# Selected LSTM after a graph network: gates i, f, g and the output gate as two sets of products, and one check of the guess behind both

## The reference

```python
def step(carry, x_t):
    h, c = carry
    logits = concatenate([h, c, x_t]) @ W_sel.T + b_sel
    s = argmax(logits)
    i, f, g, o = split(x_t @ W_ih[s].T + h @ W_hh[s].T + b_ih[s] + b_hh[s], 4)
    c2 = sigmoid(f) * c + sigmoid(i) * tanh(g)
    h2 = sigmoid(o) * tanh(c2)
    return (h2, c2), h2
```

## Time and profile before

| | us |
|---|---|
| median of three runs | 7,709.52 |
| the profiled execution | 7,713.46 |
| its span, first to last instruction | 7,711.7 |
| 256 steps with a unit (window 1,488 to 2,839) | 1,351 |
| 994 steps without (window 2,843 to 7,690) | 4,847 |

### The profile page before, as it was taken

One profiled execution on the slowest core, in us unless ns is written; L12 is line 12 of the kernel. 1 busy time (PEld: TensorE's weight loads), 2 busy tenths in 40 slices (PEclk: granted clock), 3 DMA queues, 4 the chain that ended last, 5 costly groups with the idle time before them and its releaser, 6 DMA issues. The chain is left out here.

```text
span 7711.7 us, 250693 instructions
## 1 busy us (share of the span) xinstructions
PE 6634.8 (86%) x85214; PEld 3513.4 (46%) x85215; DVE 3545.5 (46%) x16895; ACT 1004.7 (13%) x4031; POOL 945.3 (12%) x2829
## 2 busy tenths in 40 slices
PE   3467998899999998888888888888888888888888
PEld 3433444655555554444444444444444444444444
DVE  5523112355555554444444444444444444444444
ACT  0011001311111111111111111111111111111111
POOL 5703112200000000000000000000000000000000
PEclk6588998999999999999999999999999999999999
DMA  3220001622222210000000000000000000000000
GB/s 83 0 68 0 0 0 40 224 78 81 80 84 77 83 56 8 4 8 4 8 8 4 8 4 8 6 7 8 4 8 7 6 8 4 8 4 8 8 4 24
DMA packets 292938, 220.00 MB, mean 29 GB/s; under 512 B 137196, under 2 KB 268652, under 8 KB 290609
## 3 DMA queue, kind: packets, MB, share of 16 engines
q1 hardware_dynamic: 162612, 160.58, 6.2%
q10 hardware_dynamic: 106110, 59.01, 3.0%
q0 software_dynamic: 24192, 0.10, 1.0%
HBM read 160.28 MB, written 59.36 MB: 28 GB/s over the span
## 5 line engine op out<-in xcount | busy, mean ns | idle before, releaser
L1021 PE MATMUL ps<-WH,hparts 128*17 128x512 f16 x49760 | 2969.1, 380 | 148.9 <-DVE hparts L864 63.7
L1021 PEld LDWEIGHTS ps<-WH,hparts 128*17 128x17 f16 x49760 | 1305.0, 91 | 1316.2 <-DVE hparts L864 242.7
L840 DVE STREAM_TRANSPOSE gateT<-ps 128x512 f32<-128x512 f32 x1250 | 896.0, 717 | 2097.2 <-PE ps L1057 2088.0
L1091 PE MATMUL ps<-WH 128*128 128x512 f16 x4970 | 1246.1, 381 | 0.0
L467 POOL COPY xT<-hfull 128x4 f32 x1250 | 239.9, 192 | 5386.9 <-DVE hparts L862 5386.9
L1008 PE MATMUL ps<-wselT,acts 128*1 128x4 f32 x10000 | 430.5, 166 | 407.1 <-DVE acts L852 407.1
L972 PE MATMUL ps<-O,Adj 128*128 128x512 f16 x3000 | 650.3, 380 | 77.2 <-DVEq L749 77.2
L1091 PEld LDWEIGHTS ps<-WH 128*128 128x128 f16 x4970 | 404.6, 97 | 630.8 <-issue 278.7
L581 ACT ACTIVATE gateT<-gblk 128x16 f32 x1250 | 289.3, 231 | 2660.9 <-DVE pick L835 2618.4
L585 ACT ACTIVATE acts<-gates 128x16 f32<-128x16 f32 x1250 | 269.8, 216 | 2239.8 <-DVE gates L844 2239.8
L1065 PE MATMUL ps<-xT,wih_next 128*128 x2048 | 501.1, 388 | 65.1 <-DMA wih_next<-in_w_ih 34.0
(11 more groups left out here) (141 smaller groups left out, 4547.4 us busy)
## 6 DMA issues: line engine op xcount, KB each, us to landing
wih_next<-in_w_ih SPq DMA_DIRECT2D x256, 256.0 KB, 2.9
gblk<-gate_inputs ACTq DMA_DIRECT2D x48, 800.0 KB, 5.0
gate_inputs<-gx_next SPq DMA_DIRECT2D x64, 500.0 KB, 2.6
wst<-in_w_hh ACTq DMA_DIRECT2D x32, 512.0 KB, 7.6
wih<-in_w_ih SPq DMA_DIRECT2D x16, 1024.0 KB, 8.6
adjacency<-Adj SPq DMA_DIRECT2D x2, 6400.5 KB, 24.7
Adj<-adjacency SPq DMA_DIRECT2D x2, 6400.0 KB, 26.8
gate_inputs<-gstage SPq DMA_DIRECT2D x16, 500.0 KB, 6.0
```

The lines of the kernel that those rows point to most:

```text
L840: dve.transpose(gateT[:, :, 0:32], gate_ps.rearrange("p (c q) -> p c q", q=32)).then_inc(turned, 1)
L1021: nc.tensor.matmul(gate_ps[32 * j:32 * j + 17, :], hparts[:, k, :], WH[:, s * KC + k, part, j, :], start=(k == 0 and part == 0), stop=(k = ...
L1091: nc.tensor.matmul(ps[:, 2, :], WH[:, 0, 0, 0, 0:P], WH[:, 0, 0, 0, :], start=True, stop=True)
```

## The change

- PE's products are split. cell_products computes i, f and g in 384 columns (PIECES reorders WH so that the output gate is last); output_products computes the output gate in 128 columns, into another bank. hparts has two columns instead of 17.
- The branches to the code of the set now stand ahead of the logits, which are repeated in each of the four branches. The guess of the next step is loaded behind the guessed products and ahead of the wait for the pick.
- After the guessed cell products PE waits for the pick and compares. If it differs, cell and output products of the picked set follow (repeated); if not, a semaphore (settled) is raised and branches lead to the output products of the set. There is no seal: the last product of each group raises the semaphore.
- VectorE's cell waits for the guessed products and for settled, then sums rows and columns in one transposing reduction of 384 columns and adds the projected input; then it waits for the output products and does the same with 128 columns. ScalarE has a tanh of its own for the output gate. cprod follows behind both.
- WARM is 3 instead of 5. The splitting of W_hh takes three instructions where it took one. The output gate's rows of the projected input are stored last (a reordering of addresses).

```diff
     EPS = 1e-5
-    WARM = 5
+    WARM = 3
...
+    PIECES = ((0, 2 * P, 0), (2 * P, P, 3 * P), (3 * P, P, 2 * P))
...
-        gateT = sb("gateT", [P, G * SUB, 33], f32)
-        gates = sb("gates", [P, G * SUB], f32)
-        acts = sb("acts", [P, G * SUB + SUB], f32)
+        gx_now = sb("gx_now", [P, G * SUB], f32)
+        hsum = sb("hsum", [P, 3 * SUB], f32)
+        osum = sb("osum", [P, 2, SUB], f32)
+        otan = sb("otan", [P, SUB], f32)
+        gates = sb("gates", [P, 3 * SUB], f32)
+        acts = sb("acts", [P, 4 * SUB], f32)
...
-                    pool.tensor_tensor(WH[:, chunk, 1, j:j + 2, :].rearrange("p a j n -> p (a j n)"),
-                                       wst[:, b, :, :].rearrange("p j n -> p (j n)"),
-                                       WH[:, chunk, 0, j:j + 2, :].rearrange("p a j n -> p (a j n)"),
-                                       ALU.subtract).then_inc(whh_low[b], 1)
+                    for first, size, to in PIECES:
+                        part = pool.tensor_tensor(WH[:, chunk, 1, j:j + 2, to:to + size].rearrange("p a j n -> p (a j) n"),
+                                                  wst[:, b, :, first:first + size],
+                                                  WH[:, chunk, 0, j:j + 2, to:to + size].rearrange("p a j n -> p (a j) n"),
+                                                  ALU.subtract)
+                    part.then_inc(whh_low[b], 1)
...
-                    act.activation(acts[:, 0:G * SUB], gates[:, :], ACT.Tanh, scale=1.0 / GATE_SCALE).then_inc(acts_ready, 1)
-                    act.wait_ge(c_ready, act.snap(i * (2 * TG) + tl + (b * TG + 2)))
-                    act.activation(tanc[:, :], acts[:, G * SUB:G * SUB + SUB], ACT.Tanh, scale=0.5).then_inc(tanc_ready, 1)
+                    act.activation(acts[:, 0:3 * SUB], gates[:, :], ACT.Tanh, scale=1.0 / GATE_SCALE).then_inc(acts_ready, 1)
+                    act.wait_ge(osum_ready, n)
+                    act.activation(otan[:, :], osum[:, 1, :], ACT.Tanh, scale=1.0 / GATE_SCALE).then_inc(otan_ready, 1)
+                    act.wait_ge(c_ready, n)
+                    act.activation(tanc[:, :], acts[:, 3 * SUB:4 * SUB], ACT.Tanh, scale=0.5).then_inc(tanc_ready, 1)
...
-            def cell(t, n, n2):
-                dve.wait_ge(gates_mm, n)
-                dve.transpose(gateT[:, :, 0:32], gate_ps.rearrange("p (c q) -> p c q", q=32)).then_inc(turned, 1)
-                dve.wait_ge(turned, n)
-                dve.wait_ge(gx_set, n)
-                dve.tensor_reduce(gates[:, :], gateT[:, :, 0:33:16], AX.X, ALU.add).then_inc(gates_ready, 1)
-                dve.wait_ge(acts_ready, n)
-                dve.scalar_tensor_tensor(out=cprod[:, :], in0=acts[:, 0:2 * SUB], scalar=1.0, in1=acts[:, 3 * SUB:5 * SUB],
+            def cell(m):
+                dve.wait_ge(guess_mm, m)
+                dve.wait_ge(settled, m)
+                dve.tensor_reduce(hsum[:, :], gate_ps.rearrange("p (c q) -> p c q", q=32), AX.X, ALU.add,
+                                  apply_transpose=True).then_inc(turned, 1)
+                dve.wait_ge(turned, m)
+                dve.wait_ge(gx_set, m)
+                dve.tensor_tensor(gates[:, :], hsum[:, :], gx_now[:, 0:3 * SUB], ALU.add).then_inc(gates_ready, 1)
+                dve.wait_ge(ogate_mm, m)
+                dve.tensor_reduce(osum[:, 0, :], ogate_ps.rearrange("p (c q) -> p c q", q=32), AX.X, ALU.add,
+                                  apply_transpose=True).then_inc(oturned, 1)
+                dve.wait_ge(oturned, m)
+                dve.tensor_tensor(osum[:, 1, :], osum[:, 0, :], gx_now[:, 3 * SUB:4 * SUB], ALU.add).then_inc(osum_ready, 1)
+                dve.wait_ge(acts_ready, m)
+                dve.scalar_tensor_tensor(out=cprod[:, :], in0=acts[:, 0:2 * SUB], scalar=1.0, in1=acts[:, 2 * SUB:4 * SUB],
                                          op0=ALU.add, op1=ALU.mult).then_inc(cprod_ready, 1)
-                dve.tensor_scalar(osig[:, :], acts[:, 2 * SUB:3 * SUB], 1.0, float(2 ** B), ALU.add, ALU.mult).then_inc(osig_ready, 1)
-                dve.wait_ge(cprod_ready, n)
-                dve.scalar_tensor_tensor(out=acts[:, 4 * SUB:5 * SUB], in0=cprod[:, SUB:2 * SUB], scalar=0.5, in1=cprod[:, 0:SUB],
+                dve.wait_ge(cprod_ready, m)
+                dve.scalar_tensor_tensor(out=acts[:, 3 * SUB:4 * SUB], in0=cprod[:, SUB:2 * SUB], scalar=0.5, in1=cprod[:, 0:SUB],
                                          op0=ALU.mult, op1=ALU.add).then_inc(c_ready, 1)
-                dve.wait_ge(osig_ready, n)
-                dve.wait_ge(hist_free, n)
-                dve.tensor_tensor(owsel[:, :, :], osig[:, :].rearrange("p (c a) -> p c a", a=1).broadcast_to([P, SUB, S]),
-                                  wselT[:, SUB:2 * SUB, :], ALU.mult).then_inc(owsel_ready, 1)
-                dve.wait_ge(tanc_ready, dve.snap(t + 2))
+                dve.wait_ge(otan_ready, m)
+                dve.scalar_tensor_tensor(out=owsel[:, :, :], in0=otan[:, :].rearrange("p (c a) -> p c a", a=1).broadcast_to([P, SUB, S]),
+                                         scalar=1.0, in1=wselT[:, SUB:2 * SUB, :], op0=ALU.add, op1=ALU.mult).then_inc(owsel_ready, 1)
+                dve.wait_ge(hist_free, m)
+                dve.tensor_scalar(osig[:, :], otan[:, :], 1.0, float(2 ** B), ALU.add, ALU.mult).then_inc(osig_ready, 1)
+                dve.wait_ge(tanc_ready, m)
+                dve.wait_ge(osig_ready, m)
                 dve.tensor_tensor(hfull[:, :], osig[:, :], tanc[:, :], ALU.mult).then_inc(h_full, 1)
-                dve.tensor_tensor(hparts[:, :, 0], osig[:, :], tanc[:, :], ALU.mult).then_inc(h_full, 1)
-                dve.wait_ge(h_full, n2)
-                dve.tensor_tensor(hparts[:, :, 16], hfull[:, :], hparts[:, :, 0], ALU.subtract).then_inc(h_ready, 1)
-            choose(1, 2)
+                dve.tensor_tensor(hparts[:, :, 0], osig[:, :], tanc[:, :], ALU.mult).then_inc(h_high, 1)
+                dve.wait_ge(h_high, m)
+                dve.tensor_tensor(hparts[:, :, 1], hfull[:, :], hparts[:, :, 0], ALU.subtract).then_inc(h_ready, 1)
+            choose(1)
             dve.sem_inc(unit_out, 1)
             def step(t):
-                n = dve.snap(t + 1)
-                cell(t, n, dve.snap(t * 2 + 2))
-                choose(dve.snap(t + 2), dve.snap(t + 3))
-                return n
+                m = dve.snap(t + 2)
+                cell(m)
+                choose(m)
...
-            def logits(t, n):
+            def logits(n):
                 pe.wait_ge(lx_set, n)
-                pe.wait_ge(lmark_ready, n)
                 nc.tensor.matmul(logit_ps, ones[:, 0:1], lx_now[:, :], start=True, stop=False)
-                pe.wait_ge(c_ready, n)
+                pe.wait_ge(owsel_ready, n)
                 for k in range(SUB):
-                    nc.tensor.matmul(logit_ps, acts[:, G * SUB + k:G * SUB + k + 1], wselT[:, k, :], start=False, stop=False)
-                pe.wait_ge(owsel_ready, n)
+                    nc.tensor.matmul(logit_ps, acts[:, 3 * SUB + k:3 * SUB + k + 1], wselT[:, k, :], start=False, stop=False)
                 pe.wait_ge(tanc_ready, n)
                 for k in range(SUB):
                     last = nc.tensor.matmul(logit_ps, tanc[:, k:k + 1], owsel[:, k, :], start=False, stop=(k == SUB - 1))
                 last.then_inc(logits_mm, 1)
-            def products(s, n, first):
-                if first:
-                    pe.wait_ge(h_ready, n)
+            def cell_products(s, done):
                 for k in range(KC):
                     for part in range(2):
                         for j in range(4):
-                            nc.tensor.matmul(gate_ps[32 * j:32 * j + 17, :], hparts[:, k, :], WH[:, s * KC + k, part, j, :],
-                                             start=(k == 0 and part == 0), stop=(k == KC - 1 and part == 1),
-                                             tile_position=(0, 32 * j))
-            def products_of(chosen, n, first):
-                with pe.If_lt(chosen, 3):
-                    with pe.If_lt(chosen, 2):
-                        products(3, n, first)
+                            last = nc.tensor.matmul(gate_ps[32 * j:32 * j + 2, :], hparts[:, k, :], WH[:, s * KC + k, part, j, 0:3 * P],
+                                                    start=(k == 0 and part == 0), stop=(k == KC - 1 and part == 1),
+                                                    tile_position=(0, 32 * j))
+                last.then_inc(done, 1)
+            def output_products(s):
+                for k in range(KC):
+                    for part in range(2):
+                        for j in range(4):
+                            last = nc.tensor.matmul(ogate_ps[32 * j:32 * j + 2, :], hparts[:, k, :], WH[:, s * KC + k, part, j, 3 * P:4 * P],
+                                                    start=(k == 0 and part == 0), stop=(k == KC - 1 and part == 1),
```

(35 more changed lines are left out.)

85 lines of the change are left out of this document (48 added, 37 removed).

## The result

The changed kernel takes **7,883.4 us**, median of three runs (7,874.0 to 7,890.0), against 7,709.5: a ratio of 1.0224, 95% interval 1.0201 to 1.0247. It is slower by 174 us. The profiled execution has a span of 7,881.6 us against 7,711.7, a difference of 170 us.

A forecast was written before the change was run, and what follows sets the result against it. It took right tail steps as TensorE streaming, then a DVE/ACT chain; unit steps as bound by PE's program order. 7,713.5 - 100 (repeated) + 175 (unit) + 45 (repeated unit) + 10 = 7,843, said as 7,845 us; range 7,620 to 8,150.

The forecast's parts named there:

- The right step of the tail: Steps without a projection unit whose guess was right: claimed unchanged at 4.48 us, the streaming gain going into the check.
- E: Time from P at which PE's sequencer reaches the wait for the pick; forecast 0.86 us in the tail.
- R: Start of VectorE's output reduction, counted from P; forecast P+2.86 us, with the next P at R + 1.58.
- 0.44 us of streaming vanish in the check: 384 columns for 512 in the cell products gain 0.44 us, which in right tail steps goes into the check.
- The unit step: Right step beside a projection unit, issued after the output products: 5.9 against 4.92 us, +0.97 x 180 = +175 us.
- P: Start of a step's cell products; times in a step are counted from it, and a period runs to the next.
- Repeated steps: Steps whose guess was wrong: tail -0.43 us x 232 = -100 us; beside a unit +0.6 x 75 = +45 us.
- Parts at nothing: Terms put at zero: two warm products fewer, splitting W_hh in three, added DVE and ACT semaphores; likewise two weight rows for 17.
- First passage through more code: Extra time when the larger code is first run through, two first compares having taken up to 4.47 us: +10 us.
- Cheaper branches: Rival: the three branches behind the load cost less, sequencer path 0.1 to 0.3 us shorter; say 7,640 us; chance 0.14.
- Products issued one by one: Rival: small output products take 0.10 us a group, R 0.28 us later, +213 us: 8,058; chance 0.12.
- The clock falls: Rival: PE drops to 1.2 GHz under the new load, R moves by 0.9 us, +890: 8,735 us; chance 0.07.

## Why the prediction was right, and where it was off

It said 7,845, faster 0.14, slower 0.78; the time is 7,883, and the mechanism is the one it named.

**The right step of the tail.** Against the means: E 0.839 (0.86 forecast), settled 1.681 (1.69), first reduction 1.791 (1.75), first output product 2.179 (2.15), last one 2.603 (2.57), R 2.874 (2.86), period 4.511 (4.48). Between settled and the first reduction lie 0.11 us, not 0.06, but that reduction is not on the path to R. The largest misses on the path are 0.04 from settled to the first output product (0.50 for 0.46) and 0.06 behind R (1.64 for 1.58, of which 0.04 was allowed for). The result "unchanged" was 0.035 us short: 27 us of 761 steps, the largest part of what the sum missed; some 7 us of all tail steps go with the seven pieces at 1.2 GHz, taken from the steps that they touch. The claim that 0.44 us of streaming vanish in the check is shown from both sides: giving them back costs nothing as long as the check stands there (+0.045), and 0.43 us once it does not.

**The unit step.** The output products ahead of the unit, its first matmul at 3.537 (3.55 forecast) and the branch-free way back came out at 5.832 for 5.9: +165 us for +175. The way back from the ones product to the next P was 0.38 us for the 0.48 of the sum. One reason given for a term does not hold: 0.1 us less "of waits for weights and evacuation that are then covered". In neither trace does a unit wait for its weights (in the kernel before they had landed at least 5.6 us earlier), and on the way to the unit the sequencer pauses nowhere for more than 0.12 us, so that there is no such wait to cover; that 3.55 came out is in this part luck. What the prediction did not see is that the sequencer's branches behind the unit count as well, so that a load moved out of the first half came back in the second.

**Repeated steps.** In the tail -0.375 us for -0.43: -87 for -100 us. Both of its points are 0.05 late, first reduction at 3.497 (3.45) and R at 4.203 (4.15). Beside a unit the first matmul of the unit is at 4.649 instead of 4.45, and +0.775 us took the place of +0.6: +57 for +45. This term was called an estimate, of when a queue drains, and it was the roughest one.

**Parts at nothing.** The new reductions were sized right (0.583 us for 384 columns, 0.315 for 128; estimates 0.58 and 0.32). "Two rows of weights for 17 change nothing" was right of the weight loads and the product spacing, but the same edit shortened VectorE's two writes of h by 0.024 us: with 17 columns tail steps are 0.03 to 0.04 us longer and the kernel 45 us slower. First passage through more code, +10 us, came out near that: +7.5 us in the first step without a unit, -1.4 in the very first. The four terms of the sum by kind of step missed by -10, +12, +13 and +27 us; the time is 38 us above the forecast.

**The rivals.** *Cheaper branches* fell: the compare took 0.212 us in the step shown, as before. But its turning point was set too near. The sum was said to turn at a path 0.1 us shorter, with all 1,250 steps moving; the load moved back makes E 0.19 earlier in the tail and gives just the time before (0.9999). The tail moved with the path (0.206 us), the steps with a unit did not. *Products issued one by one* fell: output products start 0.0606 us a group apart, and 32 of them take 0.62 us in every row. The Trainium skill, TensorEngine Tiling (Array Packing), Instruction Overhead, gives some 60 cycles a matmul. One behind the other, 32 of them would take 0.8 us, an estimate from that figure; the trace disagrees with it for products in four column tiles, which have 0.015 us each. The small products of the logits, all in one tile, do stand 0.025 us apart, which is 60 cycles at 2.4 GHz. *The clock falls* did not occur in the sense of that rival: 24 us of the changed kernel's tail are at 1.2 GHz. One load more, or 32 more products ahead of the check, brought 0.94 to 0.97.

**Where the gain of the change lies.** In the order of issue, not in the arithmetic. The 0.65 us that the changed kernel gives away in each right step of the tail are the jump over the else paths, the taken compare and the two branches behind the check; with the check in the branch that already knows the set, the same products, reductions and semaphores run 4.7% faster than before.

## What to carry over

When work is put behind a decision, count the instructions of the engine's sequencer from the last product to the first one behind it (loads into registers 0.30 us, branches taken 0.21, branches that fall through 0.07, semaphores and gaps 0.05 each): they are not in any busy share, and taking 0.76 us of them off the path was worth 536 us here, 0.65 us in each right step of the tail and 0.39 in each beside a unit. Put the decision into the branch that already knows its answer, and an independent load where the sequencer waits anyhow; whether a place is such a one has to be read for each kind of step, since the same move gained 171 us in one version and cost 139 in the other. A saving in streaming is only worth what is late next: widen the products again on the version at hand before relying on it. And where a trace names a transfer as what ended a wait, look when the bytes that were needed had landed.

## What was not expected of the hardware

- A register load whose value is overwritten unread did not appear in the trace at all; a doubled cost has to be one that something reads.
- PE kept 2.4 GHz in the windows of the version without warm products, busy 71% of the tail. In two other versions, busy 78% and 77%, the granted clock was 0.94 to 0.97 (in the one with two loads 625 us at 1.2 GHz, in 176 pieces). The changed kernel, busy 80% of its tail, has seven pieces of 3.4 us at 1.2 GHz there. Why it fell in these and not in that one stays open.
- Writing h's two parts at a stride of 17 elements and not 2 took VectorE 0.024 us more a step (171 and 177 ns for 158 and 166).
- 32 more products ahead of a check delayed the sequencer by 0.83 us at the wait (1.49 for 0.66), not by the 0.25 us that their issue takes.
